# Half of the rows of the first three stacks issued by ScalarE, and a new job order in the lead of the last attention

## What is computed

```python
# adapter (layer 2), per batch
y = einsum('btd,bdr->btr', x, a1); y = gelu(einsum('btr,bdr->btd', y, bb1))
y = einsum('btd,bdr->btr', y, a2); x = einsum('btr,bdr->btd', y, bb2) + x
# last attention (layer 3)
h = gamma * layernorm(x) + beta
q, k, v = split(h @ Wqkv.T + bqkv)           # 16 heads of 16
att = softmax(einsum('bhqd,bhkd->bhqk', q, k), -1) / D ** 0.5
out = einsum('bhqk,bhkd->bhqd', att, v) @ Wp.T + bp
```

## Time and profile before

| | |
|---|---|
| median of three runs | 863.81 us (863.66, 863.81, 869.34) |
| the profiled execution | 867.05 us |
| its span, first to last instruction | 865.2 us |
| busy, share of the span | PE 826.3 us (95%), DVE 672.6 (78%), ACT 479.8 (55%), POOL 237.7 (27%) |
| mean granted PE clock | 0.984 |
| chain that ended last | PE 82%, DVE 9%, ACT 5% |

### The profile page before, as it was taken

One profiled execution on the slowest core, in us unless ns is written; L12 is line 12 of the kernel. 1 busy time (PEld: TensorE's weight loads), 2 busy tenths in 40 slices (PEclk: granted clock), 3 DMA queues, 4 the chain that ended last, 5 costly groups with the idle time before them and its releaser, 6 DMA issues.

```text
span 865.2 us, 13610 instructions
## 1 busy us (share of the span) xinstructions
PE 826.3 (95%) x5112; PEld 537.7 (62%) x5112; DVE 672.6 (78%) x1139; ACT 479.8 (55%) x874; POOL 237.7 (27%) x377
## 2 busy tenths in 40 slices
PE   6999999999999999999988999999999999999994
PEld 3668888988997998887866634333333333343342
DVE  7998667878658578556438989999999999999377
ACT  4746232143432443333546477888888888878760
POOL 4433512203002103111333701333333333333311
PEclk9999999999999999999989989999999999999997
DMA  8713132110000000000388700505050515000111
GB/s 309 265 50 98 50 100 100 50 52 2 1 1 1 2 1 1 1 1 1 146 149 220 294 2 3 94 21 97 24 98 24 94 23 93 21 21 21 27 36 62
DMA packets 30918, 57.43 MB, mean 66 GB/s; under 512 B 7228, under 2 KB 15152, under 8 KB 30850
## 3 DMA queue, kind: packets, MB, share of 16 engines
q1 hardware_dynamic: 25924, 50.69, 21.5%
q0 software_dynamic: 4928, 5.86, 2.9%
HBM read 39.26 MB, written 14.91 MB: 63 GB/s over the span
## 4 chain that ended last, share of the span: by engine, by line
PE 82%; DVE 9%; ACT 5%; issue 2%; POOL 1%; DMA 1%; SPq 0%; DVEq 0%; ACTq 0%
PE PA L1614 15%; PE PA L1625 15%; PE PD L1381 10%; PE PA L1359 9%; PE PD L1585 7%; PE PA L1470 5%; PE PD L1439 4%; PE PA L1426 3%; PE PD L1684 2%; DVE NMX L2156 2%; PE PA L1536 2%; PE PA L1300 2%; PE PA L1547 1%; PE PA L1460 1%; DVE ST L1782 1%
## 5 line engine op out<-in xcount | busy, mean ns | idle before, releaser
L2156 DVE TENSOR_REDUCE NMX<-PD 128x2 f32<-128x1024 f32 x256 | 301.4, 1221 | 27.7 <-PE PD L1585 23.1
L1161 ACT ACTIVATE R<-PA 128x512 f32<-128x512 f32 x512 | 267.2, 603 | 72.5 <-PE PA L1614 70.9
L1614 PE MATMUL PA<-STKR 50*128 50x512 f32 x512 | 183.7, 450 | 2.2 <-ACT R L1161 0.9
L1614 PEld LDWEIGHTS PA<-STKR 50*128 50x128 f32 x512 | 82.3, 186 | 149.9 <-ACT R L1161 137.1
L1585 PE MATMUL PD<-STKR 48*128 48x512 f32 x512 | 146.4, 450 | 2.0 <-DVE NMX L2156 2.0
L1092 ACT ACTIVATE R<-PA,VEC 128x512 f32<-128x512 f32 x64 | 43.6, 689 | 97.1 <-PE PA L1359 84.6
L1381 PE MATMUL PD<-WHR,HSR 128*128 128x256 f32 x512 | 95.0, 285 | 0.5 <-DVE HSR L2002 0.5
L1381 PEld LDWEIGHTS PD<-WHR,HSR 128*128 128x128 f32 x512 | 82.1, 191 | 5.7 <-issue 1.6
L1359 PE MATMUL PA<-XSR,WHR 128*128 128x512 f32 x256 | 80.9, 397 | 4.2 <-issue 2.0
L2001 DVE CAST HSR<-R 128x512 fp32r<-128x512 f32 x64 | 28.3, 442 | 60.0 <-ACT R L1092 60.0
L1585 PEld LDWEIGHTS PD<-STKR 48*128 48x128 f32 x512 | 60.6, 185 | 19.8 <-DVE NMX L2156 10.1
(11 more groups left out here) (319 smaller groups left out, 1289.5 us busy)
## 6 DMA issues: line engine op xcount, KB each, us to landing
STKR<-qk_terms SPq DMA_DIRECT2D x32, 384.0 KB, 8.8
R<-in_l_w SPq DMA_DIRECT2D x8, 1024.0 KB, 5.1
qk_terms<-PARTS SPq DMA_DIRECT2D x16, 512.0 KB, 4.0
W<-in_w SPq DMA_DIRECT2D x4, 1024.0 KB, 10.6
qk_terms<-PARTS SPq DMA_DIRECT2D x16, 256.0 KB, 3.9
S<-row_reciprocals POOLq DMA_DIRECT2D x56, 64.0 KB, 2.2
X<-in_x SPq DMA_DIRECT2D x4, 512.0 KB, 8.6
XT<-S POOLq DMA_DIRECT2D x56, 32.0 KB, 1.8
```

The lines of the kernel that those rows point to most:

```text
L1161: act.activation(PB[:, n % 2, j, :], PA[:, e % NEB, :], ACT.Exp).then_inc(s_exp3, 1)
L1614: pe.matmul(PA[:, e % NEB, :], KS[rows, slot(gg), jj, kt * P:(kt + 1) * P], QS[rows, slot(gg), jj, c * HALF:(c + 1) * HALF], start=True, s ...
L2156: ve.tensor_reduce(out, PD[:, o:o + NROW, :], axis=AX_X, op=ALU.max, negate=True).then_inc(s_mred, 1)
```

## The change

Two parts.

**The stacks' issue.** A new function `stack_half` issues the two DMAs of one half. For stacks 0, 1 and 2 SP issues only h = 0. ScalarE issues h = 1, in three new jobs `ks` 0, 1 and 2 (`other_rows`), after a wait for the same stored parts, and for `ks` 1 for the end of the MLP. From stack 3 on SP issues all four as before. SP's stack 2 moves behind the stores of `qk3` 8 to 11.

**The job order.** `ks` 0 stands ahead of `x2` 1 and `ks` 1 behind it. `v3` 0 moves ahead of `g` 1. Six max jobs stand ahead of `qk3` 8 instead of two: `mx` 0 and 1 behind `g`, 2 and 3 behind `bm` and ahead of `f2`, 4 ahead of `n3`, 5 behind it. `v3` 2 and 3 move from behind `n3` to ahead of it, `qk3` 7 from ahead of it to behind it. From `qk3` 8 on there are two max jobs behind each `qk3` as before, now numbers 6 to 21; `tm` 0 stands in the pair behind `qk3` 14, `ks` 2 ahead of `qk3` 13; of the `v3` jobs at the end only 4 and 7 have a max job behind them, and `mx` 24 and 25 stand behind `e0`, where it was 25 alone. The number of jobs of each kind is unchanged, but for `ks`.

```diff
-SCHED += [("x2", 1), ("vp", 0), ("qk3", 4), ("a1", 1), ("bt", 0), ("g", 1), ("v3", 0), ("qk3", 5), ("a2", 1), ("bm", 0), ("f2", 1), ("fn", 1),
...
-EARLY = 2
+SCHED += [("ks", 0), ("x2", 1), ("vp", 0), ("ks", 1), ("qk3", 4), ("a1", 1), ("bt", 0), ("v3", 0), ("g", 1), ("mx", 0), ("mx", 1), ("qk3", 5),
...
+EARLY = 6
@@
-    SCHED += [("qk3", QJOBS + j), ("mx", EARLY), ("mx", EARLY + 1)]
+    SCHED += [("ks", 2)] * (j == NPARTS + 1) + [("qk3", QJOBS + j), ("mx", EARLY)] + [("tm", 0)] * (j == QJOBS - 2) + [("mx", EARLY + 1)]
@@
-    SCHED += [("v3", TWO + j), ("mx", EARLY), ("mx", EARLY + 1) if j else ("tm", 0)]
-    EARLY += 2 if j else 1
+    SCHED += [("v3", TWO + j)] + [("mx", EARLY)] * (j % (TWO - 1) == 0)
+    EARLY += int(j % (TWO - 1) == 0)
@@
+        def stack_half(e, gg, h):
+            b, g = divmod(gg, NG)
+            k, r = g // (NG // KB), (g * GH * HD) % P
+            for side in range(2):
+                e.dma_start(STK[h * HROW:h * HROW + KSTK, slot(gg), side].bitcast(F32),
+                            DR[b, k, side, r:r + GH * HD].rearrange("(j h d) n t -> h (d n) j t", j=JJ, h=NROW)[h]
+                            ).then_inc(s_stack[gg], 16)
@@
-                    for h in range(NROW):
-                        for side in range(2):
...
+                    for h in range(NROW if gg >= NSLOT else 1):
+                        stack_half(sp, gg, h)
@@
             ones_rows(1)
+            store(range(QJOBS, QJOBS + NPARTS))
             stack(NSLOT)
             ones_rows(2)
-            store(range(QJOBS, 2 * QJOBS - 2))
+            store(range(QJOBS + NPARTS, 2 * QJOBS - 2))
@@
+            def other_rows(gg):
+                if gg == 1:
+                    act.wait_ge(s_dfull, DJ[(1, "w21", NT - 1)] + 1)
+                k = gg // (NG // KB)
+                for j in range(k * 2 * NC, (k + 1) * 2 * NC):
+                    parts_stored(act, j)
+                stack_half(act, gg, 1)
```

More of the change, by code:

```diff
@@ L121 @@
 SCHED = [x for x in SCHED if x]
-SCHED += [("x2", 1), ("vp", 0), ("qk3", 4), ("a1", 1), ("bt", 0), ("g", 1), ("v3", 0), ("qk3", 5), ("a2", 1), ("bm", 0), ("f2", 1), ("fn", 1),
-          ("qk3", 6), ("qk3", 7), ("v3", 1), ("ex", 0), ("mx", 0), ("n3", 1), ("v3", 2), ("v3", 3), ("mx", 1)]
-EARLY = 2
+SCHED += [("ks", 0), ("x2", 1), ("vp", 0), ("ks", 1), ("qk3", 4), ("a1", 1), ("bt", 0), ("v3", 0), ("g", 1), ("mx", 0), ("mx", 1), ("qk3", 5),
+          ("a2", 1), ("bm", 0), ("mx", 2), ("mx", 3), ("f2", 1), ("qk3", 6), ("fn", 1), ("v3", 1), ("v3", 2), ("v3", 3), ("ex", 0),
+          ("mx", 4), ("n3", 1), ("qk3", 7), ("mx", 5)]
+EARLY = 6
 def turn_step(m):
@@ L134 @@
 for j in range(QJOBS):
-    SCHED += [("qk3", QJOBS + j), ("mx", EARLY), ("mx", EARLY + 1)]
+    SCHED += [("ks", 2)] * (j == NPARTS + 1) + [("qk3", QJOBS + j), ("mx", EARLY)] + [("tm", 0)] * (j == QJOBS - 2) + [("mx", EARLY + 1)]
     EARLY += 2
-assert EARLY == UNIT + 2
+assert EARLY == UNIT + 6
 for j in range(TWO):
-    SCHED += [("v3", TWO + j), ("mx", EARLY), ("mx", EARLY + 1) if j else ("tm", 0)]
-    EARLY += 2 if j else 1
+    SCHED += [("v3", TWO + j)] + [("mx", EARLY)] * (j % (TWO - 1) == 0)
+    EARLY += int(j % (TWO - 1) == 0)
 SCHED += [("e0", 0)] + [("mx", n) for n in range(EARLY, LEAD)]
@@ L689, in stack @@
                     b, g = divmod(gg, NG)
-                    k, r = g // (NG // KB), (g * GH * HD) % P
+                    k = g // (NG // KB)
                     if gg >= NSLOT:
@@ L1167, in _ @@
                  "ma": modulated_tile("ma", PM, 0), "mb": modulated_tile("mb", PM, 0), "m": modulated_tile("m", PM, 0), "n1": modulated("n1", P1),
-                 "n2": modulated_tile("n2", P2, 1), "n3": last_tiles, "w3": last_weights, "v3": v3, "ex": exp_table,
+                 "n2": modulated_tile("n2", P2, 1), "n3": last_tiles, "w3": last_weights, "v3": v3, "ks": other_rows, "ex": exp_table,
                  "u0": hidden("u0", ACT.Gelu_apprx_tanh, "b1", 0), "u1": hidden("u1", ACT.Gelu, "mb1", 1),
```

## The result

Over 20 runs each the median went from 866.64 to 869.19 us: 1.0033 times the time of before, 95% interval 1.0021 to 1.0046. The forecast was 4.8 us less; 2.6 us more were measured, and 869.19 lies 3.7 us above the end of the range of 856.0 to 865.5. (The three runs of before that were shown ahead gave 863.81; over 20 runs its median lies higher.) The profiled execution of the changed kernel has a span of 866.1 us, 0.9 more than that of before. A few executions take far longer at a low granted clock (one of before_e0_filled 1227.51 us, the one of which its trace was taken); ratios and clocks leave them out.

What follows compares the result with a forecast made beforehand. PE, busy 826.3 of 865.2 us, was taken as the bound, so only filled waits could gain: 2.8 + 2.4 - 0.4 = 4.8 us, taking the median from 863.81 to 859.0 us; range 856.0 to 865.5.

Steps and rivals of the forecast that it cites:

- Job g and v3 0: Lead, before the adapter: v3 0 done first, so g starts at about 441.15 us instead of 439.44.
- The loads: Stack 0 into SBUF before mx 0 at 442.2 us; two queues taken in the upper half of 172 to 383 GB/s.
- Rival 1: Loads do not overlap: mx 0 stalls 2.9 us until 445.1, gain 1.9 us, time 861.9; chance 0.18.
- qk3 5 and a2: Behind mx 0 and 1: qk3 5 to 444.5 us, a2 at once; 1.2 us behind if half clock falls on qk3 5.
- The adds: Adapter's adds on VectorE begin only after mx 2 and 3 are reduced, at 449.3 us; before, 449.54.
- The norm: Second half ahead of n3: 1.0 us of its 1.94 excess goes, ready at 459.15 us instead of 460.32.
- n3 to qk3 8: Stretch holds 2.8 us of work, 1.4 more at half clock; qk3 8 starts 2.8 us early, between 1.5 and 4.2.
- From qk3 8 to e0: Before 29.66 us; five fewer max jobs and two or three shorter waits save 2.4 us, pattern's pace kept.
- The rows of maxima: SP issues the rows e0 needs near 481 us, ten us before e0, so e0 does not wait.
- Rival 3: e0 waits for maxima's rows behind stores and stack 2 in SP's queue; gain given back, 863.8 us; chance 0.05.
- Whatever is saved arrives whole: Steps of the last attention, 500 to 840 us, are PE-bound and unchanged, so savings ahead reach the end in full.
- rival 2: ScalarE held at its DMA issue, g 7 us late: 2.2 us slower, 866.0 us; chance 0.12.

Runs made afterwards that it cites:

- before_e0_filled: Kernel before plus six matmuls that nothing reads, two ahead of each of mx 25, 26 and 27 behind e0; ratio 0.9969 to before.
- rows_late_filled: Changed kernel with SP's stack 2 and last ones behind the maxima, plus 21 matmuls that nothing reads in PE's waits; 0.9952 of before.
- adds_free_filled: rows_late with mx 2 and 3 off the adapter's adds, exponential's table loaded behind a2, 23 unread matmuls in PE's waits; 0.9926 of before, 861.19 us.
- rows_late: Changed kernel with SP's half of stack 2 and last rows of ones issued behind the maxima and last stores; 0.9988 of before, 865.13 us.
- again: The changed kernel measured once more, no edit; 1.0032 of before, 869.03 us.
- ones_late: Changed kernel with only the last rows of ones moved behind the maxima and last stores, stack 2 left ahead; 1.0013 of before.

## Why the prediction was wrong, step by step

- **Job g and v3 0.** g forecast at 441.15, at 441.41 in a trace that runs 0.3 us late from x2 on: right.
- **The loads.** The step that failed first: the rate taken for two queues. The pieces landed 5.3 and 8.6 us (SP) and 6.0 and 9.5 us (ScalarE) after their issues, the last at 443.42, 9.9 us after the first issue. Less the 2.6 us fixed, 1.57 MB went at 215 GB/s, 1.25 times the 172 of before; I had taken it for over 1.47 times and near 383. Rival 1 (no overlap) is as far off. PE waited 0.99 us. The Trainium skill's 6% ("SBUF — State Buffer", "Can I just issue two DMAs to hit both halves?") is too low for these pieces, where it was 25%, but its warning was nearer to the trace than my estimate: 444.6 by it, 443.42 measured, where I had the stack in time for 442.2.
- **qk3 5 and a2** ran at half clock behind that wait. The chain view has 2.35 and 1.80 us where 1.5 and 1.0 were taken, 1.65 us more; I had this as the other bound, at 1.2 us.
- **The adds.** Forecast at 449.3, came at 452.4. The mechanism was the one described, VectorE reducing mx 2 and 3 first, and PE waiting for the bank (1.95 us, 1.7 forecast):

```profile
450.10 2.36 DVE NMX L2170 x2
452.46 0.61 DVE X L2135
```

- **The norm.** 2.33 us for the second half, 2.3 forecast: right. With one POOL subtraction beside it instead of two, half of the excess went.

```profile
459.82 2.33 DVE L1807 TENSOR_SCALAR XN<-X,MV,RST 128x256 f32<-128x256 f32 x4 [0.28 <-POOL RST L802]
```

- **n3 to qk3 8.** qk3 8 at 465.04 against 463.3: the delay of the adds less a full clock. (The sum's other bound, 4.2 - 1.2 - 1.4, is 1.6 and not 1.5.) From x2 on, 1.4 us were won up to here instead of 2.8.
- **From qk3 8 to e0.** The term of 2.4 us did not come at all. The changed kernel took 32.02 us for the 29.66 of before, and 2.2 of that are the wait for the rows of maxima; without it the stretch is as long as before, and so it is in rows_late_filled (29.73). Not foreseen was VectorE: ScalarE's eight copies of n3 ended at 466.65, VectorE's low parts at 467.4 and only then mx 5, so mx 7 kept PE waiting 1.42 us. I carried the pattern's pace of 4.98 us for two qk3 on from a place where VectorE was not behind. It was behind in every kernel with the new order, at full clock too (1.41 above; 0.52 in adds_free_filled, which loads the table earlier). And the turn between two max jobs made PE wait 0.27 us ahead of it and 0.79 behind it, where the sum had nothing.
- **The rows of maxima.** Rival 3, given 0.05. I put their issue near 481, pricing each of SP's issues at 0.44 us, although rows 8 had one of about 7 us right behind other pieces, and the change put two pieces and the ones directly ahead of the stores that the maxima stand behind. They were issued at 493.10, twelve us later than forecast, more than the ten that rival 3 asked for; but rival 3 priced the outcome at no change, as if the gain had been there. This step turned the balance into a loss: 3.9 us between rows_late and again.
- **"Whatever is saved arrives whole."** Wrong as a premise: from e0 to the last scores it is 345.3 us at full clock, 348.2 in before and 349.3 in the changed kernel, by how long the low clock lasts behind e0. The clock of the lead was in the sum, with bounds of 1.2 to 1.4 us either way; the stretch behind e0 was taken as unchanged, and that before itself lost 2.8 us there (and 1.7 in the last product) was not read. What sets the length of the low clock from one execution to the next stays open.
- **ScalarE held at its issue** (rival 2, 0.12): no. 0.85 and 0.79 us for each two. SP was held instead (6.83 us at 435.82).

The forecast gain of 4.8 us was thus mostly not there: at full clock the order is worth about 1 us, because the term behind qk3 8 gave nothing, and because the old order's losses were its low clock more than its idle time; it gets those back with fillings as well (0.9938).

## What to carry to other kernels

Where an order is moved, follow each small late transfer to the end of its queue: a few KB that the next stage waits for must not stand behind large loads that nobody needs yet, for both their issue and their landing. Read the granted clock behind a wait, not only in it: here the changed kernel, with 2.7 us of waiting and 14 us of half clock after its start, took 3.9 us longer behind e0 than with the wait filled. And before reordering to fill waits, fill them with matmuls that nothing reads; if that gives the same gain, the waits were dear for the clock, and the order need not be touched. A sum over one trace should also say how much of its stretch changes from one execution to the next.

## What the runs showed of the hardware

- The granted clock: six filler matmuls of 128x512 in three waits of 0.3 to 0.4 us kept it at 1.00 where it had been 0.79 over 16 us (0.9969 and 0.9952 of the time in the two groups of runs). With the waits of the lead filled too it stayed at 1.00 from 434 to 520 us in both kernels with the new order; the old order kept 3 us at 0.50.
- Four pieces of 384 KB onto 48 partitions each: 11.7 us from one queue, 9.9 us from two queues, on partitions 0 to 47 and 64 to 111 (172 and 215 GB/s once 2.6 us are taken off as fixed, an estimate from rows 9).
- An issue on SP behind other stack pieces and rows of ones took 5 to 8 us instead of 0.4 (5.13, 7.01 and 8.19 us for a store); one on ScalarE at the same moment took 0.4. Without the ones ahead it stayed short (ones_late). What the limit counts stays open, and so does which waits are needed for the clock to fall: no run took them one by one.
- Four DMAs of 4 KB landed 1.2 us after the last issue with only stores just ahead in their queue (changed), and 8.7 us after it behind two stack pieces and two stores (ones_late).
